# Maxima sent first: x loaded two batches ahead, gates behind the maxima, the maxima turned earlier in another PSUM bank

## The reference, cut to what matters

```
h = layernorm(x) * (1 + ca) + sa
q = h @ w_dq.T @ w_uq.T ; k, v = split(h @ w_dkv.T @ w_ukv.T)      # 16 heads of 16
attn = softmax(q @ k.T / 4 + causal mask) @ v
x = x + ga * (attn @ w_out.T)
h = layernorm(x) * (1 + cb) + sb
expert = argmax(h @ Wg.T)                                           # 0 or 1, per token
x = x + gb * (expert 0: gelu(h W0a + b0a) W0b + b0b,  expert 1: relu(h W1a + b1a) W1b + b1b)
```

## Time and profile before

| | |
|---|---|
| median of 3 runs (lowest, highest) | 679.35 us (678.64, 680.35) |
| the profiled execution's own time | 680.1 us |
| its span, first to last instruction | 678.3 us |
| PE busy | 560.5 us (83%) |
| DVE, ACT, POOL busy | 440.7, 367.0, 267.7 us |
| mean granted clock of TensorE | 0.872 |
| DMA | 43.87 MB; the one hardware queue 36.6% of 16 engines |
| one step in the steady part, issue to issue on SP | 37.56 us |

### The profile page before, as it was taken

One profiled execution on the slowest core, in us unless ns is written; L12 is line 12 of the kernel. 1 busy time (PEld: TensorE's weight loads), 2 busy tenths in 40 slices (PEclk: granted clock), 3 DMA queues, 4 the chain that ended last, 5 costly groups with the idle time before them and its releaser, 6 DMA issues.

```text
span 678.3 us, 14114 instructions
## 1 busy us (share of the span) xinstructions
PE 560.5 (83%) x4912; PEld 472.4 (70%) x4912; DVE 440.7 (65%) x885; ACT 367.0 (54%) x521; POOL 267.7 (39%) x268
## 2 busy tenths in 40 slices
PE   5353939899797979798897979797997979799984
PEld 4242627688686868687786868686876768778874
DVE  2463436388584949586785949495876859397463
ACT  2333625747483847467473838476474748384520
POOL 3140304245252535445442525344452525253351
PEclk9755575989797989989797979899897979799997
DMA  8806070705325170807153260808062331601100
GB/s 274 151 10 95 1 128 1 125 3 77 67 51 93 23 122 2 141 0 112 29 69 73 41 101 9 132 0 138 3 88 54 57 89 32 96 1 34 33 17 15
DMA packets 43562, 43.87 MB, mean 65 GB/s; under 512 B 5360, under 2 KB 40560, under 8 KB 43520
## 3 DMA queue, kind: packets, MB, share of 16 engines
q1 hardware_dynamic: 43520, 43.33, 36.6%
HBM read 13.39 MB, written 4.23 MB: 26 GB/s over the span
## 4 chain that ended last, share of the span: by engine, by line
PE 58%; DMA 17%; SPq 14%; issue 5%; DVE 4%; ACT 2%; POOL 0%; POOLq 0%; DVEq 0%; ACTq 0%
DMA qs<-mx_rows 14%; SPq L286 11%; PE ps_t L410 7%; PE ps_t L414 6%; PE ps_s L389 6%; PE ps_o L338 4%; PE ps_c L338 4%; PE ps_o L339 4%; PE ps_o L340 4%; PE ps_c L339 3%; PE ps_c L340 3%; PE ps_a L338 3%; PE ps_a L340 3%; PE ps_a L339 2%; PE ps_o L428 2%
## 5 line engine op out<-in xcount | busy, mean ns | idle before, releaser
L803 ACT ACTIVATE score_rows<-ps_s 128x1024 f32<-128x1024 f32 x96 | 98.8, 1030 | 92.7 <-PE ps_s L389 76.6
L816 ACT ACTIVATE p<-ps_t 128x1024 f32<-128x1024 f32 x96 | 98.2, 1023 | 70.7 <-PE ps_t L414 69.8
L1225 POOL TENSOR_SCALAR_AFFINE_SELECT score_rows<-score_rows 128x512 f32<-128x512 f32 (+1 forms) x96 | 85.2, 888 | 114.8 <-ACT score_rows L803 114.7
L943 DVE TENSOR_REDUCE mx<-score_rows 128x4 f32<-128x1024 f32 (+1 forms) x96 | 115.0, 1211 | 11.0 <-POOL score_rows L1225 11.0
L410 PE MATMUL ps_t<-qs,ks 50*128 50x256 f32 (+1 forms) x512 | 60.2, 342 | 73.0 <-DMA qs<-mx_rows 72.3
L410 PEld LDWEIGHTS ps_t<-qs,ks 50*128 50x128 f32 x512 | 44.6, 229 | 82.5 <-DMA qs<-mx_rows 49.4
L389 PE MATMUL ps_s<-ks,qs 48*128 48x256 f32 (+1 forms) x512 | 58.4, 331 | 16.4 <-DMA ks<-parts_k 14.0
L866 DVE BATCH_NORM_STATS2 ln_st<-xs 128x6 f32<-128x256 f32 (+1 forms) x64 | 23.9, 414 | 73.7 <-DMA xs<-x 69.8
L1177 POOL TENSOR_TENSOR xs<-z,xs 128x512 f32<-128x512 f32 (+1 forms) x16 | 27.7, 1733 | 104.3 <-DVE z L1015 104.3
L1168 POOL TENSOR_TENSOR ln_rs<-ln_ve,neg_half 128x2 f32<-128x2 f32 x32 | 24.1, 755 | 108.7 <-DVE ln_ve L872 108.7
L389 PEld LDWEIGHTS ps_s<-ks,qs 48*128 48x128 f32 x512 | 39.8, 205 | 34.8 <-issue 21.4
(11 more groups left out here) (160 smaller groups left out, 1650.5 us busy)
## 6 DMA issues: line engine op xcount, KB each, us to landing
qs<-parts_q SPq DMA_DIRECT2D x96, 128.0 KB, 4.3
ks<-parts_k SPq DMA_DIRECT2D x96, 128.0 KB, 5.8
xs<-x SPq DMA_DIRECT2D x16, 256.0 KB, 6.7
gates<-gates_scratch SPq DMA_DIRECT2D x16, 256.0 KB, 6.1
out<-xs SPq DMA_DIRECT2D x16, 256.0 KB, 5.6
p<-wmod SPq DMA_DIRECT2D x1, 1024.0 KB, 6.2
p<-waT SPq DMA_DIRECT2D x1, 1024.0 KB, 8.3
p<-wmod SPq DMA_DIRECT2D x1, 512.0 KB, 5.9
```

Source lines behind the costliest of these rows:

```text
L803: act.activation(score_rows[c % 2][:], ps_s[:], ACT.Copy).then_inc(scores_out, 1)
L816: act.activation(by_side, ps_t[:].rearrange("p (k h s) -> p k h s", k=2, h=n // 2), ACT.Exp, scale=SCALE).then_inc(exp_done, 1)
L943: dve.tensor_reduce(dst, score_rows[c % 2][:].rearrange("p (k h s) -> p k h s", k=2, h=n), AX_X, ALU.max).then_inc(max_done, 1)
L1225: pool.affine_select(out=diag, in_=diag, compare_op=ALU.is_ge, fill=NEG, base=0, pattern=[[0, n], [-1, P]], channel_multiplier=1).then_inc ...
```

## The change

Four edits. On SP, `load_maxima` goes ahead of `load_gates`, and the load of x goes to the end of the step and to the batch after the next. On PE, `turn_maxima` goes from the head of a step to the end of the step before, ahead of `up(at(3), 1)`, and writes the bank of the keys (`ps_b`) in place of `ps_c`; the lists of former users follow. On ACT, `maxima_rows` goes ahead of `values_copy(at(3), 1)`. No arithmetic, tile or transfer is added or taken away.

```diff
-        BANK = dict(... MT=ps_c ...)
+        BANK = dict(... MT=ps_b ...)
 # SP
                 stack_k(at(0), 0)
+                load_maxima(at(1))
                 load_gates(at(2))
-                prefetch_x(at(-1))
-                load_maxima(at(1))
                 stack_k(at(0), 1)
                 store(at(4))
+                prefetch_x(at(-2))
 # PE
-                turn_maxima(at(2), ("UP0", at(4)), ("Q", at(1)))
                 turn_values(at(3), 0, ("PVb", at(3)))
-                turn_values(at(3), 1, ("K", at(1)), ("CKV", at(1)), ("GX", at(5)))
-                up(at(4), 2, ("MT", at(2)), ("UP0", at(4)))
+                turn_values(at(3), 1, ("MT", at(2)), ("K", at(1)), ("CKV", at(1)), ("GX", at(5)))
+                up(at(4), 2, ("UP0", at(4)))
...
-                project_out(at(3), ("UP2", at(4)), ("MT", at(2)))
+                project_out(at(3), ("UP2", at(4)), ("Q", at(1)))
...
-                turn_gate(at(4), ("AT", at(3)), ("OT1", at(3)), ("K", at(1)), ("CKV", at(1)), ("GX", at(5)))
+                turn_gate(at(4), ("AT", at(3)), ("OT1", at(3)), ("MT", at(2)), ("K", at(1)), ("CKV", at(1)), ("GX", at(5)))
...
-                compress(at(0), ("GX", at(4)), ("AT", at(3)), ("OT1", at(3)), ("K", at(1)))
+                compress(at(0), ("GX", at(4)), ("AT", at(3)), ("OT1", at(3)), ("MT", at(2)), ("K", at(1)))
...
-                project_q(at(0), ("T2", at(3)), ("OP", at(3)), ("UP2", at(4)), ("MT", at(2)), ("UP0", at(4)), ("Q", at(1)))
+                project_q(at(0), ("T2", at(3)), ("OP", at(3)), ("UP2", at(4)), ("UP0", at(4)), ("Q", at(1)))
...
                 values(at(2), 3)
+                turn_maxima(at(1), ("K", at(0)), ("CKV", at(0)), ("GX", at(4)), ("AT", at(3)), ("OT1", at(3)), ("MT", at(2)), ("K", at(1)))
                 up(at(3), 1, ("DN1", at(4)), ("T1", at(0)))
 # ACT
                 gelu(at(4), 0)
+                maxima_rows(at(2))
                 values_copy(at(3), 1)
-                maxima_rows(at(2))
                 gelu(at(4), 1)
```

More of the change, by code:

```diff
@@ L208, in block_kernel @@
         ST_OF_GROUP = (2, 3, 5, 6)
-        BANK = dict(T1=ps_a, Q=ps_c, CKV=ps_b, K=ps_b, V=ps_o, MT=ps_c, OT0=ps_o, OT1=ps_b, AT=ps_b, OP=ps_c, T2=ps_c,
+        BANK = dict(T1=ps_a, Q=ps_c, CKV=ps_b, K=ps_b, V=ps_o, MT=ps_b, OT0=ps_o, OT1=ps_b, AT=ps_b, OP=ps_c, T2=ps_c,
                     GT=ps_a, GX=ps_b, UP0=ps_c, UP1=ps_a, UP2=ps_c, UP3=ps_o, DN0=ps_o, DN1=ps_a, PVa=ps_o, PVb=ps_o)
```

## The result

The changed kernel takes **639.07 us** (median of 4 runs, 632.14 to 645.24) against 679.85 us for the kernel before on the same chip: ratio 0.937, 95% interval 0.928 to 0.945. The profiled execution took 637.11 us, its span is 635.3 us. The forecast was 639 us. Medians here are over all runs of a kernel, while a ratio compares the means of its fast runs and leaves out those over 1.5% above its fastest. That the number of the forecast is so close is partly luck: two terms of the sum were off by 0.5 and 0.75 us a step, in opposite directions.

A forecast was written before the change was run, and what follows sets the result against it. Bound: a loop of SP's stack DMAs, the maxima's landing and PE's work. Twelve steps of 2.9 us (2.4 landing, 0.5 clock), plus 4.3 and 1.2 for batches 1 and 14, saved 40.3 us: 639 us, range 619 to 660.

The forecast's parts named there:

- The loop and the place of the wait: SP's stacks wait for `st_chunk`, PE's `st_chunk` 0 for the maxima: period 37.56 us, 15.39 DMA plus 22.2 PE work.
- Landing, 2.4 us a step: Maxima ahead of gates and x land 0.76 us behind the tenth stack DMA, 2.44 us earlier; bounds 1.1 to 3.2.
- Clock, 0.5 us a step: TensorE's low clock behind the shrunken 2.0 us wait costs 2.1 us a step against 2.6; bounds -0.8 to +2.6.
- Falls in most steps, here and there not: After the 2.0 us wait TensorE mostly drops to 1.2 GHz, losing 1.7 to 3.4 us, sometimes not.
- The turn on PE: Moved ahead of `up(at(3), 1)`, the turn comes 1.4 us earlier and has no wait for `k_low`, by 0.1 us.
- In fact it is needed: Without the earlier turn, SP, done with the tenth stack at 390.77, could not send the maxima: turn came at 391.20.
- x at 0: Loading x two batches ahead removes DVE's 69.8 us of waiting, said to be on no chain; costed at 0.
- Ends: Savings outside steady batches 2 to 13: batch 0 nothing, batch 1 4.3 us, batch 14 1.2, batch 15 nothing.
- The clock stays up: Rival 1: the shorter wait costs no clock, a step saves 5.0 us, 614 us; chance 0.12.
- The landing as its own latency: Rival 2: maxima's landing doesn't hang on what is ahead; only issue moves, 1.1 us a step, 662 us; chance 0.12.
- The turn's wait: Rival 4: the turn on PE waits 4.4 us for `k_low` and eats the gain, 679 us; chance 0.04.
- the late clock: Rival 3: low clock lasts into the score chunks, a step costs 3.6 us more, 717 us; chance 0.04.

The follow-up runs named there:

- SP's order alone: Kernel before with only SP's three lines changed (maxima ahead of gates, x two batches ahead and last); turn, bank and ACT's copy unmoved: 636.47 us, ratio 0.933.
- the turn alone: Changed kernel with SP's old order; only the turn, its bank and ACT's copy as changed: 680.27 us, ratio 0.999.
- Without x's move: Changed kernel with x loaded one batch ahead, between the gates and the second part of k, behind the maxima: 680.79 us, ratio 1.001.
- the filled kernel: Changed kernel plus 9 unused 512-column matmuls in PE's wait ahead of `st_chunk` 0 of batches 2 to 14: 622.95 us, ratio 0.913.
- the kernel with the maxima ahead of k: Changed kernel with the maxima also ahead of the first part of k's stack, and the gates behind its second part: 616.77 us, ratio 0.905.
- the last kernel: The 616.77 us kernel (maxima ahead of k's stack) with the next batch's `s_chunk` 0, and ACT's copy of it, moved later: 610.36 us, ratio 0.894.
- a kernel otherwise nearly the same: Kernel before with SP's order from the 616.77 us kernel (maxima ahead of k's stack), turn late in its old bank: 651.71 us, ratio 0.950.

## Why the prediction was right, point by point

- **The loop and the place of the wait.** Right. The steps end with the maxima's landing in the changed kernel too (13.5 us, then some 20 us of PE work).
- **Landing, 2.4 us a step.** Mis-sized: 15.35 - 13.48 = 1.9. The tenth stack DMA lands at 295.84 + 6.4 = 302.2, as worked out; PE begins 1.3 us behind it and not 0.8, the value of batch 0. PE's wait is 2.24 us a step on average, and not 2.0. Why the pair is slower in the steady step is open.
- **Clock, 0.5 us a step.** Mis-sized the other way: 13.8 / 11 = 1.25 us. "Falls in most steps, here and there not" was right in kind: of eleven steps four kept the clock, five had 3.4 us low and two 6.7. The two errors and a third (next point) cancel: 1.87 + 1.25 - 0.26 = 2.86 against 2.9.
- **The turn on PE.** No wait, right but for 0.11 us a step. "In fact it is needed" was wrong: SP's order alone gives 636.5 us and the turn alone 680.3. The prediction itself said why, one paragraph on: the queue is backed up until 12.2 us, so neither an issue at 6.5 nor one at 7.7 matters.
- **x at 0.** The step that failed, though the sum did not show it. The move stood in the sum as free, and what it prevents was not priced: x's landing holds `a_lo` on DVE, which was ready at 401.3 for a `project_out` at 404.3. "They are on no chain" held only for the kernel before. A cover of 3 us under a gain of 2.4, with a clock that makes `up` 3 faster as well, is no cover. Without x's move 680.8 us.
- **The rest of a step.** It grew by 0.26 us, which was missed: PE's small idle times ahead of `turn_z2` and of the turn are 2.7 of the 2.9 us.
- **Ends.** Batch 1's maxima came 12.4 us after their step's start, forecast 96.7 - 83.8 = 12.9, but k's last DMAs, behind the scratch's round trip, came later than thought: `s_chunk` 0 began at 102.76, after 3.5 us of idle, not 0.4. Up to the issue of batch 3's stacks the change saved 3.1 us, forecast 4.3. From the issue of batch 14's stacks to the end it saved 8.5 (forecast 2.9 + 1.2 = 4.1), mostly since the last two steps kept the clock.
- **Rivals.** The clock stays up (614 us): true in four of eleven steps, and the filled kernel (623 us) shows what it is worth. The Trainium skill's rule (page "TensorE: Matmul & The Clock Gate", section "HAM oscillation — how this bites in real kernels") that only longer gaps drop the clock held for those four and not for the other seven. The landing as its own latency (662): refuted by SP's order alone, where the maxima are issued when they were before and PE starts 1.9 us earlier, and by the kernel with the maxima ahead of k. The turn's wait and the late clock: did not come.

## What to carry to other kernels

When a wait on the critical path shrinks, list what lands or finishes just behind it, on other engines too, and compare its spare time with the gain: here x had 3 us for a gain of 2.4 and decided over all of it. In a backed-up DMA queue it was the bytes ahead that counted and not the moment of issue; once nothing stood ahead, it was the other way round. A PE wait of 4.4 us, and mostly one of 2.3, cost clock as well as time here, so test such a wait with filler matmuls before reordering: that took 31 of the 680 us away without touching any order. And look at the step, not only at the wait: the last kernel lost its 1.2 us wait and kept its step of 32.0 us, since DVE's `z` stood behind it.

## What the runs showed of the hardware

- A DMA on ACT's queue did not pass a backlog on SP's: no packet for 5.4 us after its issue, though its two DMAs carry 32 KB in all (2.4 to 3.4 us in three steps in which SP had issued later).
- The time at 1.2 GHz behind a wait of the same 2.3 us was 0, 3.4 or 6.7 us, so steps of one program differ by 3 us. With the clock held up by fillers the spread of the runs fell from 13 to 7 us.
- Waits of about 1.2 us left the clock up in all steady steps but one; waits of 2.2 to 2.8 us, in a kernel otherwise nearly the same, in none. Length alone does not decide: with the maxima on ACT's queue, two of eight steady waits of 2.5 to 2.8 us left it up.
